# Mamba stage: two places per chunk for h and one token tile's product with B on VectorE; linear attention one batch a step

## What is computed

```python
x = _layernorm(x + _L0_attn_ref(x, ...))    # linear attention
x = _layernorm(x + _L0_xattn_ref(x, ctx_1024, mask, ...))
x = _layernorm(x + _L0_ffn_ref(x, ...))
x = _layernorm(x + _L1_attn_ref(x, ...))    # Mamba
x = _layernorm(x + _L1_xattn_ref(x, ctx_1024, ctx_1024, ...))
x = _layernorm(x + _L1_ffn_ref(x, ...))
# linear attention, 16 heads of 16
q = elu(x Wq + bq) + 1;  k = elu(x Wk + bk) + 1;  v = x Wv + bv
out = (q (k^T v)) Wo + bo
# Mamba: 512 inner channels, 16 states
xn = x * rsqrt(mean(x * x) + 1e-6) * g;  x_s, z = split(xn W_in)
xc = silu(causal_conv4(x_s) + conv_b);  B, C, log_dt = xc W_x
dt = softplus(log_dt W_dt + b_dt);  Ab = exp(-dt exp(A_log));  bu = dt * B * xc
h = Ab * h + bu  (along the tokens);  y = sum over states of h * C
out = x + ((y + xc * D) * silu(z)) W_out
```

## Time and profile before

| what | value |
|---|---|
| median of 3 runs | 4295.16 us (4289.23 to 4302.53) |
| the profiled execution, its own time | 4285.25 us |
| its span, first to last instruction | 4283.3 us |
| mean granted TensorE clock | 0.943 |
| busy: TensorE, VectorE, ScalarE, GpSimd | 83%, 72%, 68%, 62% |
| linear attention, first transpose to last store | 14.1 to 435.8 us |
| Mamba, first to last scan | 1447.0 to 3326.9 us |

### The profile page before, as it was taken

One profiled execution on the slowest core, in us unless ns is written; L12 is line 12 of the kernel. 1 busy time (PEld: TensorE's weight loads), 2 busy tenths in 40 slices (PEclk: granted clock), 3 DMA queues, 4 the chain that ended last, 5 costly groups with the idle time before them and its releaser, 6 DMA issues. The chain is left out here.

```text
span 4283.3 us, 73949 instructions
## 1 busy us (share of the span) xinstructions
PE 3564.8 (83%) x22944; PEld 2554.7 (60%) x22976; DVE 3088.3 (72%) x5218; ACT 2933.9 (68%) x5240; POOL 2670.1 (62%) x2858
## 2 busy tenths in 40 slices
PE   7888799998964688888888888888888699994666
PEld 4555576668442366666766666666666476762333
DVE  4444688884365588788887888787887477776988
ACT  2222588873365688888888888788888377774666
POOL 0000466660065589889898999898889355552555
...
GB/s 51 39 39 34 48 43 42 42 35 104 52 30 76 33 46 53 51 46 51 51 46 51 53 49 53 51 51 46 51 42 57 34 41 43 39 36 67 50 45 35
DMA packets 199099, 204.02 MB, mean 48 GB/s; under 512 B 45742, under 2 KB 163953, under 8 KB 198788
## 3 DMA queue, kind: packets, MB, share of 16 engines
...
## 5 line engine op out<-in xcount | busy, mean ns | idle before, releaser
L2165 DVE TENSOR_TENSOR_SCAN ma_h<-ma_a,ma_pbu 128x512 f32<-128x512 f32 x1024 | 1222.7, 1210 | 323.3 <-PE ma_pbu L1763 149.5
L2061 POOL TENSOR_TENSOR ma_ch<-ma_h,ma_crep 128x512 f32<-128x512 f32 x1024 | 1335.0, 1320 | 184.5 <-DVE ma_h L2165 169.0
L1763 PE MATMUL ma_pbu<-ma_ident,ma_bu 128*128 128x128 f32 x4096 | 655.2, 284 | 171.6 <-DVE ma_h L2165 140.7
L1763 PEld LDWEIGHTS ma_pbu<-ma_ident,ma_bu 128*128 128x128 f32 x4096 | 482.3, 144 | 412.7 <-DVE ma_h L2165 287.2
L1772 PE MATMUL ma_py<-ma_ident,ma_ch 128*128 128x128 f32 x4096 | 636.2, 280 | 41.6 <-POOL ma_ch L2061 29.8
L1959 ACT ACTIVATE ma_a<-ma_dt,ma_A 128x510 f32<-128x510 f32 x1024 | 653.0, 717 | 1.0 <-issue 1.0
L1950 ACT ACTIVATE ma_bu<-ma_uT,ma_b_t 128x512 f32<-128x512 f32 x864 | 556.7, 718 | 10.6 <-PE ma_pbu L1763 8.9
L1772 PEld LDWEIGHTS ma_py<-ma_ident,ma_ch 128*128 128x128 f32 x4096 | 490.7, 145 | 69.4 <-POOL ma_ch L2061 64.4
L797 POOL TENSOR_TENSOR xa_prob<-xa_e,xa_rec_head 128x616 f32<-128x616 f32 x256 | 307.0, 1215 | 312.6 <-DVE xa_rec_head L886 312.5
L877 DVE TENSOR_REDUCE xa_top<-xa_pS 128x8 f32<-128x616 f32 x256 | 202.9, 792 | 150.3 <-PE xa_pS L566 142.3
L706 ACT ACTIVATE xa_eT<-xa_pE 77x512 f32<-77x512 f32 x512 | 276.1, 593 | 49.3 <-PE xa_pE L578 47.5
...
## 6 DMA issues: line engine op xcount, KB each, us to landing
ma_crep<-ma_ct_dram SPq DMA_DIRECT2D x256, 256.0 KB, 3.1
...
```

The costliest lines, as they stand in the source:

```text
L1763: last = pe.transpose(pbu[c % 2][:, t * P:(t + 1) * P], bu[:, s % 2, t, c * P:(c + 1) * P], ident[:, :])
L2061: pool.tensor_tensor(ch[:, s % 2, c], h[:, c], crep[:, s % 4, :], ALU.mult).then_inc(multiplied, 1)
L2165: dve.tensor_tensor_scan(out=h[:, c, :], data0=a[:, s % 2, c, :], data1=pbu[c % 2][:, :], initial=0.0, op0=ALU.mult, op1=ALU.add).then_inc ...
```

## The change

**Linear attention.** The step is one batch, and `in_turns` (a helper that other stages use) writes the first and last four out and loops over the others. In one step TensorE makes this batch's queries, the outer product of the batch before, half of this one's keys and values, the batch before's product with q, the other half, the next batch's transposes, and the projection of the batch before. PSUM has one tile for each purpose (`pX`, `pQ`, `pK`, `pM`, `pO`, `pY`). The bias matmuls and `split_in_three` go: VectorE adds the broadcast bias of keys and values (`kv_in`), GpSimd adds bo to x (`add_bias`). Values are no longer copied by ScalarE. The exp of k reads `kv_in`.

**Mamba.** h has two places per chunk; `multiplied` starts at 8; products are summed nine steps late (`LAG`). `scale_tile` moves from GpSimd's list to VectorE's, behind the scan (s, 0), as a tensor_scalar. B is turned into `pm[0]` in state 9 instead of `pm[1]` in state 7 and copied in state 10. `yv` shares the tensor of `one_av`. The places of the gates, the gated transposes, the output projection, statistics, y, one_plus, step inputs, z and u in the lists move by one to four steps.

```diff
-        h = sb("h", [P, IC, GS])
+        h = sb("h", [P, 2, IC, GS])
-        yv = sb("yv", [P, IC, GS])
+        yv = one_av
...
-                    sp.wait_ge(multiplied, K * g + (IC * s + 8))
+                    sp.wait_ge(multiplied, K * g + (IC * s + 12))
...
-                pe.wait_ge(multiplied, K * g + (IC * s + c + 5))
+                pe.wait_ge(multiplied, K * g + (IC * s + c + 9))
...
                 if t == 2 and piece == 0:
-                    if prep:
-                        pe.wait_ge(b_copied, g + 3)
-                    else:
-                        pe.wait_ge(y_ready, 2 * g + 1)
+                    pe.wait_ge(y_ready, 2 * g + 1)
...
-                        late = IC * s + c - 5
-                        if late >= 0:
-                            sum_state(g, late // IC, late % IC)
-                        if s == 0 and not first:
-                            for k in ((-1, 0), (1, 2), (3,), ())[c]:
-                                sum_state(g - 1, N - 1 if k >= 0 else N - 2, k % IC)
+                        at = IC * s + c
+                        if at < LAG and not first:
+                            late = K - LAG + at
+                            sum_state(g - 1, late // IC, late % IC)
+                        for _ in range(2):
+                            if at >= LAG + 2 and done <= at - LAG:
+                                sum_state(g, done // IC, done % IC)
+                                done += 1
...
-                pool.tensor_tensor(ch[:, s % 2, c], h[:, c], crep[:, s % 4, :], ALU.mult).then_inc(multiplied, 1)
-
-            def scale_tile(g, par, s):
-
-                if s == 1:
-                    pool.wait_ge(uT_copied, IC * g + IC)
-                pool.wait_ge(bu_turned, K * g + (IC * s + 4))
-                pool.tensor_tensor(bu[:, s % 2, TT - 1, :], uT[:, par, TT - 1, :],
-                                   b_t[:, par, TT - 1, s:s + 1].broadcast_to([P, DI]), ALU.mult).then_inc(tile_ready, 1)
+                pool.tensor_tensor(ch[:, s % 2, c], h[:, s % 2, c], crep[:, s % 4, :], ALU.mult).then_inc(multiplied, 1)
...
+            def scale_tile(g, par, s):
+
+                if s == 1:
+                    dve.wait_ge(uT_copied, IC * g + IC)
+                    dve.wait_ge(b_copied, g + 1)
+                dve.wait_ge(bu_turned, K * g + (IC * s + 4))
+                dve.tensor_scalar(bu[:, s % 2, TT - 1, :], uT[:, par, TT - 1, :], b_t[:, par, TT - 1, s:s + 1], None,
+                                  ALU.mult).then_inc(tile_ready, 1)
...
+            STATS = {(6, 1): 0, (6, 2): 1, (9, 3): 2, (10, 0): 3}
+            FINISH = {(8, 0): 0, (8, 1): 1, (11, 2): 2, (11, 3): 3}
```

VectorE's list in linear attention, one batch (new; `before` and `two_back` are the batches one and two steps earlier), and ScalarE's:

```diff
+            def batch(this, before, two_back):
+                n, p = number(*this) + 1, this[1] % 2
+                if before is not None:
+                    mask(*before)
+                dve.wait_ge(exp_done, n)
+                for f in range(C):
+                    last = dve.tensor_scalar(rq[:, p, f, :], pQ[:, f, :], bq_c[:, f:f + 1], 0.0, ALU.add, ALU.max)
+                last.then_inc(relu_done, 1)
+                if two_back is not None:
+                    finish(*two_back)
...
+                dve.wait_ge(kv_made, n)
+                dve.tensor_tensor(kv_in[:, p], pK[:, :, :], bkv_r[:, :].unsqueeze(1).broadcast_to([P, T, 2 * D]),
+                                  ALU.add).then_inc(kv_biased, 1)
+                dve.wait_ge(kv_biased, n)
+                link(dve.tensor_scalar(rk[:, p], kv_in[:, p, :, 0:D], 0.0, None, ALU.max))
+                dve.wait_ge(kexp_done, n)
+                dve.scalar_tensor_tensor(out=k[:, p], in0=ek[:, p], scalar=1.0, in1=rk[:, p],
+                                         op0=ALU.min, op1=ALU.add).then_inc(qk_ready, 1)
+                if before is not None:
+                    residual(*before)
...
+                if before is not None:
+                    attended(*before)
+                act.wait_ge(kv_biased, n)
+                act.activation(ek[:, p], kv_in[:, p, :, 0:D], ACT.Exp).then_inc(kexp_done, 1)
+                if nxt is not None:
+                    turned(*nxt)
```

476 lines of the change are left out of this document (251 added, 225 removed).

## The result

The changed kernel takes 4199.98 us (median of 4 runs, 4198.5 to 4204.0) against 4294.92 for the kernel before, a ratio of 0.9779 with a 95% interval of 0.9762 to 0.9796: 95 us faster. I had forecast 4067 and a range that ended at 4190. The gain is all in linear attention; Mamba did not get shorter.

The account below looks back on a forecast made before the run. TensorE bounds linear attention; in Mamba no single engine does, they take turns. Profiled 4285.25 less 108 (linear attention) and 120 (Mamba) gave 4057, plus 10 for the median 4067 us; own range 4015 to 4120, wider range 3970 to 4190.

Parts of the forecast that it names:

- Linear attention, gain 108: Linear attention stage: period per batch falls from 13.35 to 9.6 us, last store from 435.8 to 328; bounds 83 and 123.
- the 0.55 that I added for the chain: Linear attention: wait per batch for bias addition, exp of k and xT copy, added to TensorE's 9.05 us of work.
- h in two places: the 7.5 us go: Mamba's scans: their wait for GpSimd's multiply by C, 7.5 us per group, disappears.
- The tile: 0.6: Mamba: each tile moved to VectorE takes about 0.6 us, ten per group, so 6 us more there.
- The rival of the full lock: Mamba: each tile waits out a whole GpSimd multiply, up to 1.77 us; 122 per group, 4243 in all; chance 0.05.
- The moved places: 4.5 and 3.0 go: Mamba, per group: project_out's wait for B's copy, 4.5 us, and y's wait for rstd, 3.0 us, go.
- Sum per group 110: Mamba: a group of 118 us less 7.5, 4.5 and 3.0, plus 6 and 1, takes 110; gain 120 in all.
- Floor 103: Mamba: shortest possible group, TensorE's 102 us and 1 for the loop's turn; as a rival 3957 in all, chance 0.11.
- the waits move: Mamba: TensorE's remaining waits take what others gave, group stays near 118, only linear attention gains: 4187; chance 0.14.
- slower: Mamba: tiles wait out multiplies and GpSimd stays the bound through its stop; 126 per group, 4315; chance 0.04.
- GpSimd's stop of 8 us at the group's first sum: Mamba, step 11: GpSimd stops about 8 us with its eight places full, having 118 - 97.4 to spend.
- The signs of being wrong: Mamba: scan's wait for TensorE or ScalarE grows over 5 us per group, tile averages over 1, or group above 113.

Follow-up runs that it names:

- x21_h2_tile: Kernel before with the new linear attention, h in two places and the tile on VectorE, sums five steps late, no step moved: 4237.68 us, ratio 0.9885.

## Why the prediction was wrong

- **Linear attention, gain 108**: right. Period 9.65 for 9.6, addition 1.22 for 1.2, last store 333.9 for 328, gain 102. Of the 0.55 that I added for the chain the row shows 0.30 as idle; the rest stands in the matmuls next to it (the queries take 1.84 from start to start for my 1.72).
- **"h in two places: the 7.5 us go"**: this step failed. The wait went (in the changed kernel to 44.1 us), and by itself a longer one for TensorE came: 111.9 to 27.2 us for GpSimd, 160.1 to 290.4 for TensorE. The edit alone is 6 to 9 us slower, not 120 faster. I had priced a wait by its releaser's name. Over all its waits, VectorE was to stand 14 us less per group and stands 7.4 less. GpSimd's "own sum" of 93.4 or 104 was meant as the bound, and it is an average: in states 13 to 15 it was 21.1 of 21.7 us already.
- **"The tile: 0.6"**: mis-sized. It is 0.94 (median 0.97, 0.46 to 1.60), so 9.4 us of VectorE per group for 6. What it costs in the time of the run is less, 3.1, so this is not where the gain went. GpSimd was to pay 4 us per group in longer multiplies; their mean is 1.31 us, against 1.32 before. The rival of the full lock had 1.77 each; no tile took that. The rule of the Trainium skill behind it (SBUF — State Buffer, "SBUF: two separate sides"), that one of the two engines blocks for the other's whole instruction, would give, with this trace's durations, 0.46 alone and up to 0.46 + 1.27 beside a multiply: the trace agrees that a tile waits out what is left of one (rows under "What the tile costs"). How often a tile meets a multiply depends on the order: in x21_h2_tile, with sums five steps late, the same instruction has a median of 0.46.
- **"The moved places: 4.5 and 3.0 go"**: the waits for B's copy and rstd went, but the stretch around them, states 5 to 9, went from 39.0 to 40.7 us: two pieces of project_out were moved into it from state 4, and in a stretch where TensorE and ScalarE have 35 and 37 of 39 us there was little room; no run moves them back. I also costed the gates at nothing. They left states 0 and 1, where TensorE was the fullest in the group shown, for states 2 to 4, where 19.9 us of VectorE's work stood in 21.2; four gates of 0.63 and three tiles of 0.94 make that 25.2 (measured 24.7), and the stretch became 26.6. All of this could be worked out from windows of the trace of before.
- **"Sum per group 110"**: 119.7. Floor 103: the sum over stretches of the fullest engine, 112 before and 115 after, is a closer bound on a group as it stands. It is none on what another order of the lists can reach, and the finer the cut, the closer it comes to the length itself.
- **The rivals**: "the waits move", with its 4187, is the nearest in time, and I gave it 0.14. Its account is half right: for h alone the wait moved to TensorE as it says, but in the changed kernel VectorE's idle time did fall, and the longer work on VectorE took it. "The lock in full" at 4243 has the wrong size, "slower" at 4315 did not come.
- **GpSimd's stop of 8 us at the group's first sum**: it is 4.4 and 1.7, and harmless as I said. That the late sums would make GpSimd wait 278 us I did not see; no run shows that it costs anything.
- **The signs of being wrong**: of the three only "a group stays above 113" came. The scan's wait for TensorE grew by 1.1 us per group and the tile averages 0.94, both within what I had allowed.
- In total: the spans differ by 4283.3 - 4196.7 = 86.6, which is 102 from linear attention less 15 in Mamba. The medians differ by 95, since the profiled execution of before was 10 us below its median and that of the changed kernel 1.5.
